# A selective-scan layer on one core: the side work of a unit put at other steps

## Time and profile before

| what | value |
|---|---|
| median of 3 runs | 1246.59 us (1246.4 to 1247.64) |
| the profiled execution | 1246.36 us, its span 1244.6 us |
| busy, DVE | 1089.3 us, 88% of the span |
| busy, PE | 1064.5 us, 86% |
| busy, POOL | 1024.0 us, 82% |
| busy, ACT | 870.6 us, 70% |
| granted TensorE clock, mean | 0.943 |

### The profile page before, as it was taken

One profiled execution on the slowest core, in us unless ns is written; L12 is line 12 of the kernel. 1 busy time (PEld: TensorE's weight loads), 2 busy tenths in 40 slices (PEclk: granted clock), 3 DMA queues, 4 the chain that ended last, 5 costly groups with the idle time before them and its releaser, 6 DMA issues.

```text
span 1244.6 us, 13235 instructions
## 1 busy us (share of the span) xinstructions
PE 1064.5 (86%) x3786; PEld 635.6 (51%) x3786; DVE 1089.3 (88%) x1220; ACT 870.6 (70%) x1581; POOL 1024.0 (82%) x679
## 2 busy tenths in 40 slices
PE   6688998988898888989987988998899898887997
PEld 4345555555455455555554554554555455443454
DVE  2898999898999989999989899989899998878684
ACT  4687687676777775876767777758767767657653
POOL 4598988978889879889889798898898897858674
PEclk9899999899999999999989999989999989988899
DMA  7222223222222221222221322212222322334351
GB/s 179 93 102 78 84 83 104 83 84 86 75 103 77 90 95 68 87 99 85 83 104 57 103 84 84 103 59 108 78 84 83 103 80 90 102 115 164 107 179 28
DMA packets 64538, 116.79 MB, mean 94 GB/s; under 512 B 34218, under 2 KB 47954, under 8 KB 64466
## 3 DMA queue, kind: packets, MB, share of 16 engines
q1 hardware_dynamic: 64466, 115.96, 27.4%
HBM read 108.47 MB, written 7.47 MB: 93 GB/s over the span
## 4 chain that ended last, share of the span: by engine, by line
ACT 33%; PE 32%; DVE 23%; issue 10%; POOL 2%; DVEq 0%; DMA 0%; POOLq 0%; ACTq 0%; SPq 0%
PE Yp L785 15%; DVE SCAN L1111 13%; ACT DA L513 6%; DVE SCAN L1076 5%; PE PP L797 3%; PE PP L810 3%; PE PP L866 2%; ACT L541 2%; ACT L529 2%; ACT UDT L535 2%; DVE GATES L1157 2%; POOL SCAN L448 2%; DVE VV L1087 2%; ACT DAS L521 2%; PE PP L818 2%
## 5 line engine op out<-in xcount | busy, mean ns | idle before, releaser
L448 POOL TENSOR_TENSOR SCAN<-SCAN,CS 128x768 f32<-128x768 f32 x384 | 692.4, 1817 | 121.7 <-DVE SCAN L1111 120.6
L1111 DVE TENSOR_TENSOR_SCAN SCAN<-DA,CAR,SCAN 128x384 f32<-128x384 f32 x672 | 638.8, 1002 | 54.6 <-ACT DA L513 54.6
L785 PE MATMUL Yp<-SCAN,IDENT 128*128 128x384 f32 x1536 | 597.7, 516 | 72.4 <-DVE VV L1087 70.9
L513 ACT ACTIVATE DA<-UDT,A 128x384 f32<-128x384 f32 x672 | 377.9, 578 | 257.0 <-DVE SCAN L1111 256.9
L785 PEld LDWEIGHTS Yp<-SCAN,IDENT 128*128 128x128 f32 x1536 | 297.0, 201 | 260.4 <-POOL SCAN L448 89.3
L1076 DVE TENSOR_TENSOR SCAN<-UDT,BB 128x768 f32<-128x768 f32 x240 | 224.9, 937 | 19.8 <-PE BB L767 19.7
L456 POOL TENSOR_TENSOR SCAN<-UDT,BS 128x768 f32<-128x768 f32 x96 | 173.9, 1812 | 0.0
L926 PE MATMUL PP<-XN,WT 128*128 128x384 f32 x352 | 124.4, 486 | 1.4 <-ACT ZB L626 1.4
L767 PE MATMUL BB<-PT,SEL 96*128 96x384 bf16 x288 | 98.2, 341 | 7.4 <-DVE DA L1076 4.4
L926 PEld LDWEIGHTS PP<-XN,WT 128*128 128x128 f32 x352 | 66.6, 189 | 48.5 <-issue 1.9
L468 POOL TENSOR_TENSOR UDT<-UDT 128x768 f32<-128x768 f32 x23 | 41.7, 1814 | 52.7 <-DVE UDT L1161 52.7
(11 more groups left out here) (212 smaller groups left out, 1233.9 us busy)
## 6 DMA issues: line engine op xcount, KB each, us to landing
CS<-bc_rows SPq DMA_DIRECT2D x96, 768.0 KB, 4.0
BS<-bc_rows SPq DMA_DIRECT2D x24, 768.0 KB, 6.1
out<-XN SPq DMA_DIRECT2D x32, 192.0 KB, 2.5
X<-in_x SPq DMA_DIRECT2D x24, 192.0 KB, 3.6
X<-in_L_ffn_memory_tokens SPq DMA_DIRECT2D x16, 256.0 KB, 2.9
XN<-in_L_ffn_memory_tokens SPq DMA_DIRECT2D x16, 256.0 KB, 3.0
bc_rows<-XDT SPq DMA_DIRECT2D x24, 48.0 KB, 1.5
X<-in_L_ffn_memory_router SPq DMA_DIRECT2D x1, 512.0 KB, 4.3
```

Source lines behind the costliest of these rows:

```text
L448: pool.tensor_tensor(M[:, n1 % MRING], HB[:, n1 % HRING], over_halves(CS[:, n1 % CRING]), ALU.mult).then_inc(m_ready, 1)
L513: act.activation(DA[:, h, 0:T], DT[:, par, h], ACT.Exp, scale=A[:, h, n:n + 1])\
L785: last = pe.matmul(Yp[:, h, 0:T], IDENT[:, :], M[:, n3 % MRING, h], start=n3 == 0, stop=n3 == NS - 1)
L1111: dve.tensor_tensor_scan(HB[:, s % HRING, h], factor, term, CAR[:, ds(J * NS * HALVES + s * HALVES + h, 1)], ALU.mult, ALU.add).then_inc(s ...
```

## The change

The arithmetic is the same but for the order of work. `AHEAD` becomes states 14 and 15; their decays are made at steps 10 and 11 of the same unit. The side work is put at other steps:

- conv 9 to 12 and the Silu excursion at 13 (for unit J + 2, and z of J); x projection 14; B and C copied (`copy_rows`) and the first LESS matmul (`take_high`) at 15; the second LESS matmul 0, the parts 1, dt projection and Abs, Relu 2, the fit 3 to 10, dt 11, dt u 12. So a unit is prepared one unit earlier than before, and in unit 0 two steps later (`late`).
- norm: mean 4, subtraction 5, variance 6, Ln 7, `normalize` 10.
- back: VV 2, output projection 3, copy 4, mean and subtraction 5, variance 7, Ln 8, POOL 11 and 13. z projection 8, its copy 9. D times u 4.
- the router five steps earlier (3 to 9), the memory blocks at other steps; SP writes the rows of unit J + 2 at the end of `spread(J)`.

The diff, cut to its core (line numbers of waits and tiles not shown are unchanged):

```diff
-AHEAD = (1, 2)
+AHEAD = (14, 15)
...
-        MIX = {(COMB - 1, 9): (0, 0), (COMB - 1, 10): (0, 1), (COMB - 1, 11): (0, 2), (COMB - 1, 12): (0, 3),
+        MIX = {(COMB - 1, 9): (0, 0, 1), (COMB - 1, 10): (0, 1, 2), (COMB - 1, 11): (0, 2, 4),
...
                 sp.wait_ge(hi_ready, f + 1)
+                if f >= 2:
+                    sp.wait_ge(c_loaded[1], 16 * (GROUPS // 2) * (f - 1))
                 sp.dma_start(ROWS_D[p], XDT[XROW0:DTROW, :]).then_inc(rows_written, 16)
...
+            def spread(J, par):
+
+                load_c(J, par, 1)
+                if J == 0:
+                    write_rows(1, 1)
+                load_c(J, par, 2)
+                load_c(J, par, 3)
+                if J == ROUTE:
+                    sp.wait_ge(idx_ready, 1)
+                    gather(0)
+                load_b(J + 1, 1 - par)
+                load_c(J + 1, 1 - par, 0)
+                write_rows(J + 2, par)
 
...
-                if front and s == 11:
+                if front and s == 9 + late(J):
...
-                if norm and s == 15:
+                if norm and s == 10:
...
+            def copy_rows(u):
+
+                act.wait_ge(xp_ready, u + 1)
+                act.wait_ge(rows_written, 16 * u)
+                act.activation(XDT[XROW0:XROWS, :], PP[XROW0:XROWS, 1, 0:T], ACT.Copy)
+                act.wait_ge(parts_ready, u)
+                act.activation(PART[:, :], PP[0:DTROW, 1, 0:T], ACT.Copy).then_inc(hi_ready, 1)
...
-                    if front and s >= NS - len(AHEAD):
-                        act.wait_ge(dt_ready, J + 2)
-                        decay_ahead(J + 1, 1 - par, s - NS + len(AHEAD))
+                    if s in (10, 11):
+                        decay_ahead(J, par, s - 10)
...
+                if main and s == 13:
+
+                    act.preload_act_table_set("silu_and_others")
+                    if conv:
+                        act.wait_ge(ysum_done, NS * J + 3)
+                        for h in range(HALVES):
+                            act.wait_ge(conv_ready, 2 * c + h + 1)
+                            last = act.activation(U[:, par, h], PP[:, h, 0:T], ACT.Silu, bias=CB_[:, h:h + 1])
+                        last.then_inc(u_ready, 1)
+                    if main:
+                        act.wait_ge(z_copied, J + 1)
+                        positive(act, v_ready, J)
+                        act.activation(GZ[:, :, :], ZB[:, :, :], ACT.Silu).then_inc(gz_ready, 1)
+                    act.preload_act_table_set("natural_log_exp_and_others")
...
+                if main and s == 9:
+
+                    act.wait_ge(z_ready, J + 1)
+                    act.activation(ZB[:, :, :], PPT, ACT.Copy).then_inc(z_copied, 1)
+                if back and s == 4:
+
+                    act.wait_ge(op_ready, k + 1)
+                    act.activation(unit_x(k).rearrange("p q t -> p (q t)"), PP[:, 0, 0:T], ACT.Copy).then_inc(x2_ready, 1)
+                if front and s == 0 + late(J):
+
+                    act.wait_ge(res_ready, f + 1)
+                    act.activation(PART[:, :], PP[0:DTROW, 1, 0:T], ACT.Copy).then_inc(mid_ready, 1)
+                if front and s == 1 + late(J):
+
+                    act.wait_ge(res2_ready, f + 1)
+                    act.activation(PT[:, fp], PP[0:DTROW, 1, 0:T], ACT.Copy).then_inc(parts_ready, 1)
+                if conv and s == 15:
+                    copy_rows(c)
+                if at(J, 0) and s == 1:
+                    copy_rows(1)
+                if front and s == 2 + late(J):
 
                     act.wait_ge(dtp_ready, f + 1)
                     positive(act, dt_ready, f)
                     act.activation(SE[:, :, :], PPT, ACT.Abs).then_inc(sp_chain, 1)
                     act.activation(DT[:, fp], PPT, ACT.Relu).then_inc(relu_done, 1)
+                if front and s == 3 + late(J):
                     act.wait_ge(sp_chain, 3 * f + 1)
                     act.activation(SE[:, :, :], SE[:, :, :], ACT.Exp, scale=-1.0).then_inc(sp_chain, 1)
-                if front and s == 8:
+                if front and s == 4 + late(J):
 
...
-                if back and s == (11 if main and not norm and not front or at(J, COMB - 1) else 10):
+                if back and s == 8:
                     act.wait_ge(var2_ready, k + 1)
...
-                for i in range(len(AHEAD)):
-                    decay_ahead(0, 0, i)
+                act.preload_act_table_set("silu_and_others")
+                for h in range(HALVES):
+                    act.wait_ge(conv_ready, 2 + h + 1)
+                    last = act.activation(U[:, 1, h], PP[:, h, 0:T], ACT.Silu, bias=CB_[:, h:h + 1])
+                last.then_inc(u_ready, 1)
+                act.preload_act_table_set("natural_log_exp_and_others")
...
+            def project(u, upar):
+
+                pe.wait_ge(u_ready, u + 1)
+                for h in range(HALVES):
+                    last = pe.matmul(PP[0:XROWS, 1, 0:T], XPT[:, h], U[:, upar, h], start=h == 0, stop=h == 1)
+                last.then_inc(xp_ready, 1)
+
+            def take_high(u):
+
+                pe.wait_ge(hi_ready, u + 1)
+                pe.matmul(PP[0:DTROW, 1, 0:T], LESS[:, 0], PART[:, :], start=False, stop=False,
+                          skip_group_check=True).then_inc(res_ready, 1)
...
+                if conv and s == 15:
+                    take_high(c)
+                if at(J, 0) and s == 1:
+                    take_high(1)
+                if front and s == 0 + late(J):
+
+                    pe.wait_ge(mid_ready, f + 1)
+                    pe.matmul(PP[0:DTROW, 1, 0:T], LESS[:, 1], PART[:, :], start=False, stop=True,
+                              skip_group_check=True).then_inc(res2_ready, 1)
+                if front and s == 2 + late(J):
+
+                    pe.wait_ge(hi_ready, f + 1)
+                    if at(J, ROUTE + 1):
+                        pe.wait_ge(f_dve, 9)
+                    for h in range(HALVES):
+                        if h == 1:
+                            pe.wait_ge(parts_ready, f + 1)
+                        last = pe.matmul(PP[:, h, 0:T], DTW[DTROW:XROWS + 1, h], XDT[DTROW:XROWS + 1, :],
+                                         start=True, stop=True, tile_position=(DTROW, 0))
+                    last.then_inc(dtp_ready, 1)
+
+                if main and s == 4:
 
                     for h in range(HALVES):
                         pe.matmul(Yp[:, h, 0:T], DD[:, h], U[:, par, h], start=False, stop=False)
 
...
-                if back and s == 4:
+                if conv and s == 14:
+                    project(c, par)
+                if at(J, 0) and s == 0:
+                    project(1, 1)
+                if back and s == 3:
 
                     pe.wait_ge(v_ready, k + 1)
                     if front:
...
-                if norm and s == 9:
+                if norm and s == 4:
...
-                if main and s == z_step(J, norm):
-
-                    if at(J, COMB - 1) or at(J, COMB):
-                        pe.wait_ge(xc2_ready, k + 1)
-                    elif back:
+                if main and s == 8:
+
+                    if back:
                         pe.wait_ge(ln2_done, k + 1)
...
-                if conv and s >= 13:
-
-                    if s == 13:
+                if conv and 9 <= s < 13:
+
+                    if s == 9:
...
-                if back and s == LAG:
+                if back and s == LAG - 1:
...
-                if norm and s == 10:
+                if norm and s == 5:
```

More of the change, by code:

```diff
@@ L65, in da_index @@
 def da_index(unit, n):
-    return (NS - len(AHEAD)) * unit + (n if n < AHEAD[0] else n - len(AHEAD))
+    return (NS - len(AHEAD)) * unit + n - sum(1 for m in AHEAD if m < n)
 def pool_index(n):
@@ L465, in step @@
                         .then_inc(xh2_done, 1)
-                if front and s == 12:
+                if front and s == 12 + late(J):
                     pool.wait_ge(dt_ready, f + 1)
@@ L605, in step @@
                         .then_inc(fac1_square, 1)
-                if front and s == 10:
+                if front and s == 8 + late(J):
                     act.wait_ge(fac1_square, f + 1)
@@ L814, in step @@
                               start=False, stop=True, skip_group_check=True).then_inc(op_ready, 1)
-                if back and s == 6:
+                if back and s == 5:
                     pe.wait_ge(x2_ready, k + 1)
@@ L819, in step @@
                     last.then_inc(mean2_ready, 1)
[L821 to L825 removed]
+                if back and s == 7:
                     pe.wait_ge(sq2_ready, k + 1)
@@ L887, in step @@
                     last.then_inc(mean_ready, 1)
-                if norm and s == 11:
+                if norm and s == 6:
                     pe.wait_ge(sq_ready, g + 1)
@@ L929, in step @@
                             last.then_inc(conv_ready, 1)
-                if front and s == 4:
-                    pe.wait_ge(hi_ready, f + 1)
```

(18 more changed lines are left out.)

135 lines of the change are left out of this document (40 added, 95 removed).

## The result

| | median us | lowest to highest, runs | granted clock |
|---|---|---|---|
| before | 1246.49 | 1244.99 to 1247.64, 4 | 0.943 |
| after | 1369.10 | 1362.55 to 1371.02, 4 | 0.933 |

The account below looks back on a forecast made before the run. DVE sets the time: 44.85 us of work plus waits of 1.9, 2.7 and 1.4 make 50.85 a unit against 47.46. 68 us for 20 units, 8 clock, 5 unit 0 and 3 last units sum to 84: 1330 us, range 1262 to 1380.

Parts of the forecast that it names:

- What bounds it, and the decays: DVE sets the time; its waits for decays, 54.6 us before, were taken as none, bounds 0 and 1.9 us.
- DVE's work: DVE's operations in a unit, same in number and size: 45.0 us less 0.15 for a drained passage, 44.85.
- wait of VV: DVE's VV waits for PE's sum of state 15, behind ACT's copies: 1.9 us, bounds 0 and 2.7.
- XC of norm, with the spread of state 6: DVE waits for PE's mean behind Relu and the output projection: 2.7 us, 0.35 on the spread; bounds 1 and 3.5.
- spread of state 11: DVE waits for this spread, behind PE's z projection, which waits for Ln of `back`: 1.4 us, bounds 0 and 2.5.
- clock: PE's lower clock behind idle stretches: 0.4 us a unit, 8 us in all, between 0 and 2.2 a unit.
- The fit and the table loads: ACT's fit goes from four busy steps to ten; loads of 1.28 us let the step 13 excursion fit between decays.
- rival 2: Half clock behind every gap on PE: 2.2 us a unit, 44 instead of 8, 1366 us; chance 0.15.
- I count nothing for it: POOL: Dt is ready at step 12 as before, its order gets lighter, cover is steps 13 to 15; no cost.
- The ends: Unit 0 costs 5 us more; the last three units 3 us more, between -8 and +15.
- Rival 1: Faster: PE so far behind that it finds its operands there and DVE runs unbroken; 55 less, 1191 us; chance 0.12.
- Rival 3: Half of it: ACT gets ahead, waits come to 3 us instead of 6; 1262, with some clock 1270 us; chance 0.15.

Follow-up runs that it names:

- keep_busy: The changed kernel with four more f32 matmuls, results never read, in PE's step 15 ahead of `take_high`: 1327.3 us.
- e4_dt_at_12: The changed kernel with DVE's last two operations on dt at step 12 instead of 11: 1309.4 us.
- e1: The changed kernel with ACT's three copies of B and C one step earlier: 1300.8 us.
- e2: The changed kernel with Abs and Relu ahead of the decay of state 3 in ACT's step 2: 1299.0 us.
- e3: The changed kernel with the z projection at step 9, behind the spread of state 11, and the convolution at 10 to 13: 1303.0 us.
- the four repairs: The changed kernel with one edit each, `e1`, `e2`, `e3` and `e4_dt_at_12`: 1300.8, 1299.0, 1303.0 and 1309.4 us.
- all4: The changed kernel with the edits of `e1`, `e2`, `e3` and `e4_dt_at_12` together: 1194.1 us.
- pool_product_early: The changed kernel with POOL's dt u queued one step earlier, ahead of its product M of state 11: 1329.5 us.
- old_with_fit_spread: The kernel before with only ACT's softplus fit spread over steps 8 to 12 and dt one step later: 1228.1 us.

## Why the prediction was right in kind and short in size

**What bounds it, and the decays.** Right. DVE sets the time, and its waits for decays fell from 54.6 us to 1.3.

**The three waits.** Right in place, in cause and in order. In size, by the unit shown above:

| term of the sum | foretold | measured |
|---|---|---|
| DVE's work | 44.85 | 46.17 |
| wait of VV | 1.9 | 2.82 |
| XC of norm, with the spread of state 6 | 2.7 | 4.18 |
| spread of state 11 | 1.4 | 1.45 |
| clock | 0.4 | in the two waits above: 1.28 + 1.61 |
| unit | 51.25 | 54.6 |

The walks through the queues were good: at the higher clock VV waits 1.54 us (`keep_busy`) against 1.9 foretold, and XC with its spread 2.57 (`e4_dt_at_12`) against 2.7. Unit 1 of the changed kernel, where nothing is slowed by the clock, takes 51.74 us against 51.25. The repairs confirm the causes: `e1`, `e2` and `e3` each took away the wait it was aimed at (`e2` 1.54 of its 2.40 us).

**A row read wrongly.** The 0.39 us from ACT's copy to its matmul is no handover. The matmul of 540.70 in the earlier trace rows has no idle time ahead of it: PE was still busy with the sum in front of it. Where PE does wait, after, the matmul starts 0.05 us behind the end of the copy (638.08 to 638.13) and of Ln, and 0.14 behind Relu. With 0.05 for 0.39 my walk gives about 1.5 us for VV, and 1.54 was measured at the higher clock.

**The fit and the table loads.** The fit has eight steps after (3 to 10), and not the ten of my text, with one operation in each; that changed no term. The excursion at step 13 held up nothing, as foretold: a load takes 1.28 us, ACT's next operation starts at once (683.39 to 684.68), and behind the excursion ACT waits 2.48 us for DVE.

**The clock: the term that was mis-sized most.** I gave it 0.4 us a unit; it is 2.9, by `keep_busy` and by the projections of the four repairs, more than the 2.2 of rival 2. It falls on 18 of the 20 ordinary units and not on some, as in the kernel before. The Trainium skill's warning (TensorE: Matmul & The Clock Gate, HAM oscillation), that waits between bursts of matmuls make each burst start at the lower rate, held for two of the chains from unit 3 on, and I should have given it more weight than one row of a unit that was no faster for its gap. In the page's example the waits are for transfers and longer than the 2.05 and 2.69 us here. Against it stand unit 1 and the projection of `e4_dt_at_12`, at the higher rate behind the same gaps.

**"I count nothing for it": the step that failed.** This I said of POOL, whose order I had looked at only for when its results are due, not for what it runs beside. The addition of dt takes 2.32 us in the mean instead of 0.96, with 0.11 won back on the operation ahead of it: 1.25 a unit, 29 us over 23, the very rise of DVE's busy time (1089.3 to 1118.6). POOL's rows after:

```profile
675.62 1.00 POOL L466 TENSOR_TENSOR XC<-XC,RSTD 128x384 f32<-128x384 f32 x1
676.58 2.52 POOL L450 TENSOR_TENSOR SCAN<-SCAN,CS 128x768 f32<-128x768 f32 x1
```

Lay them beside DVE's two rows of 675.93 and 677.53 above. They alternate: DVE's operation ends 0.8 us after POOL's XC has ended (676.6 to 677.4), POOL's product 1.7 us after that (679.1), DVE's addition 0.8 after that (679.9), each a little under its length alone (0.93, 1.82, 0.96). In `all4` POOL's product starts first, at 591.33, and is not slowed at all; DVE's takes the whole delay:

```profile
591.33 1.81 POOL L450 TENSOR_TENSOR SCAN<-SCAN,CS 128x768 f32<-128x768 f32 x1
```

```profile
591.85 2.11 DVE L1170 SCALAR_TENSOR_TENSOR GATES<-GATES 128x768 f32<-128x768 f32 x1
```

591.33 + 1.81 + 0.93 = 594.07 against an end at 593.96. The Trainium skill (SBUF — State Buffer, Who interferes with whom) has this as a rule: a DVE instruction with two operands in SBUF and a GpSimd instruction that reads SBUF exclude each other, and the one that starts first keeps the port to its end. The trace agrees, and it shows the other half too: the products with B, the scans and XC of DVE, which take one of their operands from PSUM, are never lengthened beside POOL (0.92 to 0.96, 0.98 to 1.02 and 0.53 to 0.56 us each, in all the kernels here). In a unit only the two operations on dt are exposed. In the kernel before the first of them already stood beside POOL's XC (1.55 us); the change moved the second beside a product of POOL.

**The base.** An error of the sum that went the other way. I took 51.25 - 47.46 for each unit, but 47.46 is the undisturbed one; every fourth and fifth takes 50.5 and 49.15, and the mean is 48.64. By my own numbers I should have had 2.6 and not 3.8 us a unit (with the clock): 24 us less. The rise of the ordinary units, 114.9 us against 76 foretold, is thus short by 63 us in the units after and too long by 24 in those before. The 63 are 3.1 a unit, by the table 3.4 less 0.2 for the first two units, which are shorter; the 3.4 are 1.3 of DVE's work, 2.5 of clock more than I had, less 0.4 by which the waits at the higher clock are below mine.

**The ends.** Unit 0 with what lies ahead of it: 9.3 foretold as 5. The waits of DVE up to there show 4.5 us for XC of norm, 1.5 for VV of unit 1, and 2.4 more in the prologue than before. The last three units: 0.1 against 3, inside its bounds.

**The rivals.** Rival 1, faster, needed PE so far behind that its waits for ACT fall away; it kept them (58.7 us at `take_high`). It was not far in the code, however: with the three waits mended and the addition as well, `all4` stands at 1194 us, and 1191 is what that rival gave. That the two are so close is chance: the rival's units are 44.9 us, those of `all4` 46.3, and its last three units are 10 us shorter, which no rival had. Rival 3 fell with the size of the waits. Rival 2 was right on the clock and gave 1366, near the 1369 measured, but without the 1.25 us of POOL and with the wrong base; its closeness is partly chance.

**What stays open.** What in a unit decides which chain gets the lower clock. The same gaps of 2.69, 2.05 and 2.29 us have none of their chains slowed in unit 1 after, and two of them from unit 3 on; `e3` and `e4` have the projection at the higher rate behind the same gap, `pool_product_early` has it by turns, and in `e1` and `keep_busy` the slow matmuls move to another chain. No run here sorts that out.

## What to carry to other kernels

When a schedule is moved, write down beside which operation of POOL each DVE operation with both operands in SBUF comes to stand, not only when results are due: here that cost 1.25 us a unit, and one change in POOL's order, a product queued behind the wait instead of ahead of it, was worth 33 us. Such a loss is in no list of waits; it shows in the mean length of the operation and in the engine's busy time. An idle time that is not there matters too: a start without one says nothing of how long a handover takes. A matmul that waits for another engine in an in-order queue is priced with what stands behind it, at both levels of the clock; an edit elsewhere in the period can move a chain from one to the other (here 1.3 or 1.6 us each). And a rise per unit is taken against the mean unit, not against the undisturbed one.

## What the runs showed that I had not expected

- Four more f32 matmuls a unit on the busiest but one engine made the kernel 42 us faster (1369.1 to 1327.3), by keeping the clock at 1.00 through the chain that DVE waits for (1.7 us a unit in the mean, 2.9 in half of the units).
- DVE and POOL operations that exclude each other take 2.32 and 2.52 us instead of 0.96 and 1.82; one that starts behind POOL's takes 2.01 instead of 0.93. The largest part of what `old_with_fit_spread` gains is of this kind and not a wait.
- Four repairs in four different places brought the same 1.61 us at a place that three of them don't touch (`e2` starts that projection earlier), by the clock of one group of matmuls: 2.88 us before the repair and 1.61 with it, in all units of two of them, 18 of 20 of the third and 11 of 20 of the fourth.
- A periodic kernel settles: from the third unit on each took 54.61 us within 0.03, with the lower clock at the same two places; the first two, with the same gaps, took 51.74 and 52.86.
